# Inner products of a DLRM interaction: one quarter's eight samples interleaved in PSUM, and copied out in runs of eight

## The reference, cut to what matters

```python
x = layer_norm(dense_t @ Wd.T, gd, bd)                    # (512, 128)
y = layer_norm(einsum('bnd,ed->bne', sparse_t, Ws), gs, bs)
y = layer_norm(einsum('bne,pn->bep', y, Wsi), gsi, bsi)   # (512, 128, 32)
T = concatenate([x[:, None, :], swapaxes(y, 1, 2)], axis=1)   # (512, 33, 128)
Z = einsum('bnd,bmd->bnm', T, T)                          # (512, 33, 33)
out = layer_norm(Z[:, TRIL_I, TRIL_J] @ Wl.T, gl, bl)[:, :384]
h = relu(concatenate([out, dense_t], 1) @ W_top1 + b_top1)
y = relu(h @ W_top2 + b_top2) @ W_top3                    # (512, 1)
```

## Time and profile before

| what | value |
|---|---|
| median of 3 runs | 186.32 us (186.28 to 187.85) |
| span of the profiled execution, first to last instruction | 185.4 us |
| around the span (median of the runs less the span) | 0.9 us |
| PE, DVE, ACT, POOL busy | 80%, 70%, 58%, 56% of the span |
| mean granted TensorE clock | 0.936 of full speed |

### The profile page before, as it was taken

One profiled execution on the slowest core, in us unless ns is written; L12 is line 12 of the kernel. 1 busy time (PEld: TensorE's weight loads), 2 busy tenths in 40 slices (PEclk: granted clock), 3 DMA queues, 4 the chain that ended last, 5 costly groups with the idle time before them and its releaser, 6 DMA issues.

```text
span 185.4 us, 4668 instructions
## 1 busy us (share of the span) xinstructions
PE 148.0 (80%) x1825; PEld 113.2 (61%) x1825; DVE 130.1 (70%) x300; ACT 106.9 (58%) x245; POOL 104.3 (56%) x111
## 2 busy tenths in 40 slices
PE   0089877977969947459996978899799799977995
PEld 0084544434549544419794947569596666877994
DVE  6269659772959594908697999579799967943142
ACT  1202435594868486866667877585877857831230
POOL 3778777877878777777777777777840000020000
PEclk9999999996999669855999999999999999997899
DMA  5816334141111112311111123111111100110000
GB/s 153 294 33 194 137 58 161 32 139 26 34 21 29 24 28 61 61 27 27 28 33 23 32 58 64 28 28 25 28 25 40 33 7 11 27 38 0 0 0 0
DMA packets 6003, 9.59 MB, mean 52 GB/s; under 512 B 2303, under 2 KB 3538, under 8 KB 5854
## 3 DMA queue, kind: packets, MB, share of 16 engines
q0 software_dynamic: 3392, 3.45, 10.3%
q1 hardware_dynamic: 2232, 5.08, 9.1%
q10 hardware_dynamic: 358, 0.78, 1.1%
HBM read 8.01 MB, written 0.00 MB: 43 GB/s over the span
## 4 chain that ended last, share of the span: by engine, by line
PE 40%; ACT 23%; DVE 19%; issue 11%; DMA 5%; ACTq 1%; DVEq 0%
PE psB L318 11%; ACT Zs L639 10%; DVE B L831 4%; ACT U L600 4%; DMA dense_sb<-in_dense 4%; PE psG L284 4%; DVE qA L809 4%; DVE prod L802 3%; PE psZ L333 3%; PE psW L352 3%; PE psU L299 3%; DVE ssB L838 3%; ACT sdB L617 2%; PE psB L520 2%; PE psZ L424 2%
## 5 line engine op out<-in xcount | busy, mean ns | idle before, releaser
L257 POOL DMA_INDIRECT g_sb<-in_table,row_id x104 | 102.8, 989 | 31.7 <-issue 31.4
L831 DVE TENSOR_TENSOR B<-psB,bias 128x512 f32<-128x512 f32 x31 | 20.0, 686 | 26.2 <-PE psB L318 26.2
L639 ACT ACTIVATE Zs<-psZ 32x264 f32<-32x264 f32 x59 | 36.3, 616 | 2.1 <-PE psZ L333 1.0
L318 PE MATMUL psB<-U,ws_g 64*128 64x512 f32 x64 | 20.9, 735 | 15.3 <-ACT U L600 15.2
L611 ACT ACTIVATE sqB<-B 128x512 f32<-128x512 f32 x31 | 19.1, 632 | 23.1 <-DVE B L831 23.1
L299 PE MATMUL psU<-wsi_x,g_sb 128*128 128x192 f32 (+4 forms) x128 | 23.3, 330 | 7.3 <-DVE g_sb L824 7.3
L299 PEld LDWEIGHTS psU<-wsi_x,g_sb 128*128 128x128 f32 x128 | 20.9, 206 | 11.1 <-DVE g_sb L824 11.0
L284 PEld LDWEIGHTS psG<-gram,sT 128*128 128x128 f32 x104 | 14.0, 207 | 14.5 <-ACT sT L587 10.0
L850 DVE TENSOR_TENSOR T<-B,rB 128x512 f32<-128x512 f32 x31 | 21.5, 692 | 1.1
L838 DVE TENSOR_REDUCE ssB<-sqB 128x16 f32<-128x512 f32 x32 | 21.7, 677 | 0.1
L284 PE MATMUL psG<-gram,sT 128*128 128x128 f32 x104 | 17.2, 308 | 0.7 <-ACT sT L587 0.7
(11 more groups left out here) (159 smaller groups left out, 226.7 us busy)
## 6 DMA issues: line engine op xcount, KB each, us to landing
g_sb<-in_table,row_id POOLq DMA_INDIRECT x104, 2.5
wl_sb<-in_wl SPq DMA_DIRECT2D x1, 1280.0 KB, 6.0
w_sb<-in_w SPq DMA_DIRECT2D x2, 512.0 KB, 5.4
w_sb<-in_w SPq DMA_DIRECT2D x1, 768.0 KB, 4.5
small_sb<-in_small SPq DMA_DIRECT2D x1, 615.5 KB, 4.1
dense_sb<-in_dense ACTq DMA_DIRECT2D x1, 512.0 KB, 7.3
Zt<-Zs SPq DMA_DIRECT2D x3, 80.0 KB
Zt<-Zs SPq DMA_DIRECT2D x3, 70.0 KB
```

Of the source, the lines that this page charges most:

```text
L257: pool.indirect_dma_start(g_sb[:, k, h * DSP:(h + 1) * DSP], None, table, bass.IndirectOffsetOnAxis(row_id[:, 2 * k + h:2 * k + h + 1], 0) ...
L318: pe.matmul(psB[h][:, :], ws_g[h * DSP:(h + 1) * DSP, :], U[h * DSP:(h + 1) * DSP, u % 2, :], start=not (last and h == 0), stop=True).then ...
L639: act.activation(to, product, ACT.Copy).then_inc(Z_kept, 1)
L831: dve.tensor_tensor(B[:, h, :].rearrange("p (s j) -> p s j", j=PROJ), psB[h][:, :].rearrange("p (s j) -> p s j", j=PROJ), bias[:, :].rearr ...
```

## The change

The matmul of sample n writes its 33 columns to PSUM columns n, n+8, n+16, ... (a step of 8 elements, 32 bytes), so that a quarter's eight samples are interleaved: PSUM has for each column c a run of 8 samples. The copy then reads 264 elements in a row, and writes 33 runs of 8 neighbouring elements (32 bytes each), the runs 256 bytes apart. The place of every number in `Zs`, the counts of instructions, their order and all waits are the same. The copies on DVE go through the same function.

```diff
         def z_places(u, gq):
             b, lo = u // BU, 2 * US * (u % 2) + GQ * gq
             bank = psZ if u < UNITS - 1 else psU
-            return (Zs[:, b % 2, u % BU // 2, 0:COLS, lo:lo + GQ].rearrange("p c s -> p s c"),
-                    bank[gq * PROJ:(gq + 1) * PROJ, 0:GQ * COLS].rearrange("p (s c) -> p s c", s=GQ))
+            return (Zs[:, b % 2, u % BU // 2, 0:COLS, lo:lo + GQ],
+                    bank[gq * PROJ:(gq + 1) * PROJ, 0:GQ * COLS].rearrange("p (c s) -> p c s", s=GQ))
...
-                            mm = pe.matmul(bank[gq * PROJ:(gq + 1) * PROJ, n * COLS:(n + 1) * COLS],
+                            mm = pe.matmul(bank[gq * PROJ:(gq + 1) * PROJ, n:GQ * COLS:GQ],
                                            T[:, u % 2, h, s, 2:2 + PROJ], T[:, u % 2, h, s, 0:COLS],
                                            start=True, stop=True)
```

## The result

The changed kernel takes 178.6 us (median of 4 runs, 178.24 to 181.37) against 186.3 for the kernel before beside it (4 runs, 185.39 to 187.85): ratio 0.962, 95% interval 0.956 to 0.968. The forecast was 181.1, so the direction was right and the gain, 7.7 us, was 2.5 larger than its 5.2; the time lies 0.2 under the low end that I gave. The profiled execution has a span of 177.1 us and took 178.9.

What follows compares the result with a forecast made beforehand. The bound was taken as the latency of one unit's loop round the engines, none near full. Gains of 1.80, 0.27 and 2.64 us (4.7) plus 0.5 at the end gave 5.2 off 186.3: 181.1 us, range 178.8 to 186.8.

Steps and rivals of the forecast that it cites:

- The price of the copy: The copy to Zs (L639) falls from 616 to 395 ns, 0.22 us saved, on DVE's three as well.
- Rival 3: The copy does not change, 33 runs being as dear as 264 elements: 186.3 us; chance 0.08.
- The matmul's write: The inner products (L333) writing PSUM with a step cost nothing more: taken at 0.
- Rivals 1 and 2: L333's stepped write: half pace, at most 0.35 us a unit, chance 0.17; serial, up to 193.7 us, chance 0.13.
- Ordinary steps, 0.30 each: ACT ahead of U: fourth copy 0.22, copies two and three 0.08, first nothing; 1.80 us over six units.
- The three steps with all four copies, 0.88 each: Steps 7, 9 and 11: all four ACT copies count, 0.88 us for each of units 8, 10, 12; 2.64 in all.
- not by 13: Sign: ACT's busy time down by 13 us (61 x 0.22) while the span falls by 5.
- The end, 0.5: The last four ACT copies, one behind another after the loop: 0.5 us gained, reaching L397.
- small terms, 11 and 15: Units 11 and 15: gains capped by their lateness at 0.18 and 0.09 us, 0.27 together.
- unit 7, which was to gain nothing: Units 4, 7 and 13 gain nothing, because PE hides the copies.
- rival 4, the clock: The end's shorter wait keeps the clock full there: 179.5 us, or 178.6 with one project too; chance 0.12.
- the two that I had named as a sign of being wrong: The forecast is wrong if the low-clock slices, eight in the profile before, move by more than two.

Runs made afterwards that it cites:

- e3: The changed kernel with the dense part's 512-column matmuls also writing PSUM with a step of 8 and their copies reading so; 178.86 us, one execution.
- before again: The kernel before, unchanged, profiled once more; 182.52 us, with a span of 180.7 us.
- changed again: The changed kernel, unchanged, profiled once more; 178.94 us, ratio 0.9605 to the kernel before.
- e2: The changed kernel with its stepped matmul write kept and the copy put back to sample by sample; 185.32 us, ratio 1.001 to the kernel before.
- e9: The kernel before with the new layout only in units 14 and 15; 182.85 us, ratio 0.985.
- e10: The same run as before again: the kernel before, unchanged; 182.52 us.

## Why the prediction was right or wrong

- **The price of the copy** (395 ns, from neighbours' copies): right, 378. I had stayed at 390 and above because no row was faster per element; the extrapolation from 256 to 264 elements (390) was 3% too high. The reason, single-element writes 256 bytes apart, is shown by the pair copy alone (378) and matmul alone (617), with the copy of `e3` as a check on the order. Rival 3 is dead.
- **The matmul's write** (taken at 0): right, 200 against 202 ns, and at 512 columns 592 against 593. Rivals 1 and 2 are dead. They should have had less than the 0.30 that I gave them, but the rows of before could not say so.
- **Ordinary steps, 0.30 each:** in full-clock periods of old and new copies units 9 and 14 gained 0.19 and 0.32, unit 2 0.31 (9.38 to 9.07). The first copy gained nothing there and U waits in five units: the mechanism stands.
- **The three steps with all four copies, 0.88 each:** the term that was too large, 2.64 in the sum. Units 8, 10 and 12 gained 0.44, 0.30 and 0.68 between before again and changed again, 1.42 in all. Two errors. First, I multiplied four by the difference of the durations. Behind these copies ACT starts the next instruction before the copy's record has ended, where that one does not read PSUM: in step 11 of before the first copy starts at 129.68, and `deviation_b` behind it at 130.10, 0.42 later, though the copy's record is 0.61 long; in the changed kernel it is 0.29 (124.48 to 124.77), for a record of 0.38. The start of the successor is what counts, and it moves by 0.13 there, and by 0.24 only in front of something that reads PSUM (0.64 to 0.40). From start to start the four copies of step 11 bring 0.12, 0.25, 0.10 and 0.23, which is the 0.7 that unit 12 gained; in step 7 the fourth, too, stands in front of an instruction that reads SBUF, and the four bring 0.58. (Unit 8's 0.44 is less because its first copy began 0.14 earlier in before again; it began at the same place in the first profile of before, 9.71, and the gain there is 0.55.) Second, unit 10 is an ordinary unit: its first copy waits for PE in the trace on which I worked, and starts without a wait in before again and in both profiles of the changed kernel; that wait is no part of the step as such. The same overlap is why ACT's busy time fell by 8.4 us and not by 13. The row behind the 0.42, from the kernel before:

```profile
130.10 0.26 ACT L617 ACTIVATE sdB<-ssB,eps_c 128x16 f32<-128x16 f32 x1
```

- **The changed kernel's step 11**, for comparison with the earlier trace rows:

```profile
124.48 0.38 ACT L639 ACTIVATE Zs<-psZ 32x264 f32<-32x264 f32 x1 [0.31 <-PE psZ L333]
124.77 0.29 ACT L617 ACTIVATE sdB<-ssB,eps_c 128x16 f32<-128x16 f32 x1
125.08 0.79 ACT L639 ACTIVATE Zs<-psZ 32x264 f32<-32x264 f32 x2
125.22 1.26 PE L299 MATMUL psU<-wsi_x,g_sb 128*128 128x160 f32 x8
125.78 0.29 ACT L617 ACTIVATE sdB<-ssB,eps_c 128x16 f32<-128x16 f32 x1
126.77 0.59 ACT L600 ACTIVATE U<-psU 128x512 f32<-128x512 f32 x1
```

  Mix ends at 125.22 + 1.26 = 126.48 and U starts at 126.77: late by 0.29 where it was 0.95.
- **The end, 0.5:** right, 28.5 to 28.0 with the clock full in both.
- **Together:** the copies bring 2.2 in units 8 to 15 and 0.5 at the end, both measured at full clock. For units 2 to 7 the cleanest pairs of periods at hand give 0.31, 0.21 (9.05 in e2), 0.08 (7.76 in e9), 0.36 (9.48 in e9), about 0.3 and 0.27 (7.86 in e10), 1.5 in all. That is 4.2 us where the prediction had 5.2. Of the small terms, 11 and 15 together gained 0.28, as written; unit 7, which was to gain nothing, gained 0.27, and unit 3 gained 0.21 instead of 0.30.
- **The rest of the 7.7, about 3 us,** is in the main rival 4, the clock, which I had given 0.12 and priced at 1.5 to 2.5, and the late copy of step 9. The low-clock slices went from eight to five, and four of the eight are back at full clock, more than the two that I had named as a sign of being wrong. The sum had two errors of opposite sign: the copies brought a fifth less than it said, and the clock, which it had at nothing, brought more than that back. With the copies alone the time would have been about 182.1 (186.3 - 4.2). The clock should have been part of the forecast's own range on the fast side: the profile on which I worked had 23.7 us at half clock. What is shown: over 41 executions the changed kernel has 8.4 us less at half clock, for which the common line gives 2.6 us, and it lies 4.3 us lower at equal clock, next to the 4.2 from the periods; the slow stretch at the end, 1.5 us, came in four of six profiles with old end copies and in none of eight with the short ones; and the late copy, 0.56 us in unit 10, stands in five of seven profiles with old copies, the first of before among them, and in none of the changed kernel's two. What is not shown: why the clock stays up. That shorter ACT lists shorten PE's waits ahead of such stretches is argued, and the 2.39 us wait without a slow stretch speaks against waits alone.

## What to carry to other kernels

When a copy is slower per element than its neighbours of the same shape, look at the order of its write to SBUF before anything else; going through the elements in another order on both sides, with the producer left alone, gave here all that the larger change gave. Count a shortened instruction by when its successor can start, in each place of the list: ahead of an instruction that then waits for another engine it is worth nothing, and ahead of one that already started before the record's end it is worth less than the difference of the durations. And profile the kernel before twice: two profiles of one program differed by 4.7 us, more than the whole effect of the copies.

## What the hardware showed that I had not expected

- A copy from PSUM to SBUF of 32 x 264 fp32 that writes runs of 8 costs 378 ns on ACT and 430 on DVE whether it reads PSUM in a row or with a step of 33 elements, and 616 or 617 and 612 or 613 whether it reads in a row or with a step of 8, if it writes single elements 256 bytes apart. Only the written side counts. The Trainium skill (SBUF — State Buffer, Specifications (TRN2)) asks for two hits in a 16-byte line; runs of 8 fp32 agree with full pace, single ones with the loss. No run here tried a run of two.
- A matmul's write to PSUM with a step of 8 fp32 is free here, at 33 columns in four column groups at once (200 against 202 ns, 196 in both for the last unit) and at 512 columns (592 against 593).
- Behind a copy to `Zs` ACT begins its next instruction before the copy's record ends if that one reads SBUF, 0.09 us before behind a short copy (start to start 0.29 for a record of 0.38) and 0.2 us before behind a slow one (0.42 for 0.61), and not if it reads PSUM (0.40 for 0.38, and 0.64 for 0.62). It is no rule for ACT at large: behind the copy of U (L600) the next instruction, L587, reads PSUM too and starts 0.10 us before that record's end (0.49 for 0.60). What decides it is open.
